# Second and third layer normalisation: the elementwise pass on ScalarE with a scale and a bias for each token

## The chip, the cores and the metric

One core of a Trainium2 chip runs the whole program. The metric is the device time of one execution in microseconds (us). The engines are named as the profile names them: PE is TensorE (matrix multiply), PEld its weight load, DVE is VectorE, ACT is ScalarE, POOL is GpSimd, SP is SyncE, which here only issues DMAs.

## What is computed

2048 tokens (2 batches of 1024) of width 128 go through a feed-forward layer, an attention layer and the same feed-forward layer again; each has a normalisation of x ahead of it and a residual addition behind it. Cut to what matters:

```python
def _layernorm(x, axis=-1, eps=1e-05):
    m = jnp.mean(x, axis=axis, keepdims=True)
    v = jnp.var(x, axis=axis, keepdims=True)
    return (x - m) / jnp.sqrt(v + eps)

x = x + 0.5 * ffn(_layernorm(x), gate_weight, gate_up_proj, down_proj)
x = x + attn(_layernorm(x), W_kv_down, W_k_up, W_v_up, W_q, W_q_rope, W_k_rope, W_o)
x = x + 0.5 * ffn(_layernorm(x), gate_weight, gate_up_proj, down_proj)
```

`ffn` routes each token to the 8 best of 32 experts (logits = x @ gate_weight.T, top 8, softmax weights), gathers up to 128 tokens for each expert, applies the expert and adds the weighted results back to the tokens. `attn` is causal attention with 16 heads, whose keys and values come from a compressed state c_kv = x @ W_kv_down.

## The kernel before, in words

Tokens lie on the 128 partitions, in 16 tiles (`NT`) of 128 tokens, so that x is a tile [128, 16, 128]. The 16 tiles are handled in 4 groups (`NG`) of 4 tiles (`TG`). Each engine has its own program, written out by hand in its final order; the engines wait for each other through semaphores (`wait_ge`, `then_inc`). An engine works strictly in the order of its program, so an instruction that waits holds everything behind it on that engine.

A normalisation m (0, 1, 2) of group i is this on DVE: `stat` (L794, four bn_stats), `moment` (L800, four bn_aggr, which give mean and variance into `mv`), `variance` (L806, adds eps, increments `var_ready`), then on ACT `root` (L539, square root of 4 numbers for each partition into `sd`), then on DVE `norm`: a reciprocal (L812) into `rstd`, and four tensor_scalar (L818), one for each tile, that write xn = (x - mean) * rstd and increment `xn_ready`. The function `front(m)` interleaves these for the first and third normalisation: the norm of group i comes behind the variance of group i+1, and the norm of group 3 stands not in it but in `route(k)` (L914), between `best(k, 0)` and `choice(k, 0)`. The second normalisation is interleaved with the residual additions (`add`, L785) in the loop at L1039 to L1050.

Behind the second normalisation (`transposes(1, xn, compress)` on PE, `transposed(1, after=compressed)` on ACT):

- PE transposes a group of xn (L1182, waits for `xn_ready`) into PSUM, ACT copies it out as `xnT` (`turned_out`, L545), PE multiplies by W_kv_down (`compress`, L1429), ACT copies that out as `ckvT` (`compressed`, L674). PE's order is transpose 0, transpose 1, compress 0, transpose 2, compress 1, transpose 3, compress 2, compress 3, and the transpose of group i waits for the copy of group i-2. PE goes on with `rope` (L1438) only when all four `ckvT` are there.
- ACT's order in this stretch is root of groups 0 to 3 (L667, L668), then the copies.
- A block of matmuls on zeros (`idle_work`, L1172) stands on PE ahead of these transposes.

Behind the third normalisation (k = 1 from here on):

- ACT's order (L740 to L764): roots 0 and 1, `turned_out` of group 0, root 2, `first_part` 0 (L559, the bf16 copy of xn), root 3, `turned_out` 1, `copy_logits` 0 (L563), a table load for Exp with a small activation (`table_for`, L530), `first_part` 1, `turned_out` 2, `copy_logits` 1, `second_part` 0 (L569), and so on.
- PE transposes xn and computes the router's logits for each group (L1200) as soon as `xnT` is there, with a few idle matmuls between.
- DVE's `route` does for each group: `rest_of` (L824, xn minus its bf16 copy), `best` (L833 and L836, top 8 of the logits, waits for `lg_copied`), `choice` (L841, L842, the mask from which PE counts positions). It ends in `active` (L857 to L863), which gives the number of tiles to gather, and `still_hots` (L894), the one-hot matrices that PE's first gather (L1256) takes.
- POOL's `split(1)` (L445) makes the third bf16 part of xn behind `second_part`.

`split_done` counts POOL's splits; the wait for `NG` of it keeps xn of the second normalisation from being written before the first layer has split its own. `x`, `mv`, `rstd` and the new tile are SBUF tiles that stay for the whole kernel.

Of the kernel before, what the change touches and what calls it, by code (L numbers as in the profile page):

```python
# [10 lines left out]
ALU = mybir.AluOpType  # L11
ACT = mybir.ActivationFunctionType
AX = mybir.AxisListType

P = 128
B, T, D = 2, 1024, 128
N = B * T
NT = N // P
# [17 lines left out]
NG = 4  # L36
TG = NT // NG
# [52 lines left out]
ORDER = ((0, 1, 2, 3), YORDER, (0, 1, 2, 3))  # L90
# [16 lines left out]
def build(nc, x_in, w_kv_down, w_k_up, w_v_up, w_q, w_q_rope, w_k_rope, w_o,  # L107
# [3 lines left out]
    def sb(name, shape, dt=F32, stack=None):  # L111
        return (stack or ctx).enter_context(nc.sbuf_tensor(name, shape, dt))

    def sem(name):
        return ctx.enter_context(nc.semaphore(name))
# [11 lines left out]
    with ctx:  # L127
# [7 lines left out]
        x = sb("x", [P, NT, D])  # L135
        xn = sb("xn", [P, NT, D])
# [15 lines left out]
        mv = sb("mv", [P, NT, 2])  # L152
        var = sb("var", [P, NT])
        sd = sb("sd", [P, NT])
        rstd = sb("rstd", [P, NT])
        wat = sb("wat", [P, 5, D])
        wrope = sb("wrope", [P, 2, DR])
        wswap = sb("wswap", [P, 2, DR])
# [105 lines left out]
        w_stored = sem("w_stored")  # L264
        w_back = [sem(f"w_back{c}") for c in range(RING, NCH)]

        stat_done, moments, var_ready, sd_ready, rstd_ready, xn_ready = (
            sem(n) for n in ("stat_done", "moments", "var_ready", "sd_ready", "rstd_ready", "xn_ready"))
        turned, xnT_ready, logits_done = sem("turned"), sem("xnT_ready"), sem("logits_done")
        part0, rem1, part1, split_done = sem("part0"), sem("rem1"), sem("part1"), sem("split_done")  # L270

# [248 lines left out]
        def _(e):  # L520
# [13 lines left out]
            def root(m, i):  # L534

                g = ORDER[m][i]
                t = slice(g * TG, (g + 1) * TG)
                e.wait_ge(var_ready, m * NG + i + 1)
                e.activation(sd[:, t], var[:, t], ACT.Sqrt).then_inc(sd_ready, 1)  # L539

            def turned_out(n, i):

                g = YORDER[i] if n == 1 else i
                e.wait_ge(turned, n * NG + i + 1)
                e.activation(xnT[:, g * BANK:(g + 1) * BANK], ps[:, i % RING, :], ACT.Copy).then_inc(xnT_ready, 1)  # L545

            def transposed(n, after=None):
                for g in range(NG):
                    turned_out(n, g)
                    if after and g >= 1:  # L550
                        after(g - 1)
                if after:
                    after(NG - 1)

            def first_part(k, g):

                t = slice(g * TG, (g + 1) * TG)
                e.wait_ge(xn_ready, 2 * k * NT + (g + 1) * TG)
                e.activation(xp[:, t, 0, :], xn[:, t, :], ACT.Copy).then_inc(part0, 1)  # L559

            def copy_logits(k, g):
                e.wait_ge(logits_done, k * NG + g + 1)
                e.activation(flat(lg[:, g * TG:(g + 1) * TG, :]), ps[:, LBANK[k][g % RING], g * TG * E:(g + 1) * TG * E], ACT.Copy).then_inc(lg_copied, 1)  # L563
# [75 lines left out]
            root(0, 2)  # L639
            first_part(0, 0)  # L640
            turned_out(0, 1)
            root(0, 3)
            copy_logits(0, 0)
# [22 lines left out]
                e.activation(stacked[rows, :], sq[rows, 0, rows], ACT.Copy).then_inc(units_stacked, 1)  # L666
            for g in range(NG):  # L667
                root(1, g)  # L668
            e.wait_ge(w_stored, 32 * (NCH - RING))

            def compressed(i):
# [68 lines left out]
            table_for(ACT.Sqrt)  # L740
            transposed(2)
            root(2, 0)
            root(2, 1)
            turned_out(3, 0)
            root(2, 2)
            first_part(1, 0)
            root(2, 3)
            turned_out(3, 1)
            copy_logits(1, 0)
            table_for(ACT.Exp)  # L750
# [17 lines left out]
        def _(e):  # L768
            e.sem_inc(added, RING)

            def tiles(g):
                return range(g * TG, (g + 1) * TG)

            def group(g):
                return slice(g * TG, (g + 1) * TG)
# [32 lines left out]
            def norm(m, i):  # L808

                g = ORDER[m][i]  # L810
                e.wait_ge(sd_ready, m * NG + i + 1)
                e.reciprocal(rstd[:, group(g)], sd[:, group(g)]).then_inc(rstd_ready, 1)  # L812
                e.wait_ge(rstd_ready, m * NG + i + 1)
                if m >= 1:

                    e.wait_ge(split_done, NG)
                for t in tiles(g):
                    e.tensor_scalar(xn[:, t, :], x[:, t, :], mv[:, t, 0:1], rstd[:, t:t + 1],  # L818
                                    ALU.subtract, ALU.mult).then_inc(xn_ready, 1)

            def rest_of(k, g):

                e.wait_ge(part0, k * NG + g + 1)
                e.tensor_tensor(rem[g][:, :, :], xn[:, group(g), :], xp[:, group(g), 0, :], ALU.subtract).then_inc(rem1, 1)  # L824
# [4 lines left out]
            def best(k, g):  # L829

                e.wait_ge(lg_copied, k * NG + g + 1)
                for t in tiles(g):
                    e.max(t8[:, t, :], lg[:, t, :]).then_inc(top8, 1)  # L833
                e.wait_ge(top8, k * NT + (g + 1) * TG)
                for t in tiles(g):
                    e.match_replace(rep[:, t, :], t8[:, t, :], lg[:, t, :], LOWEST).then_inc(replaced, 1)  # L836

            def choice(k, g):

                e.wait_ge(replaced, k * NT + (g + 1) * TG)  # L840
                e.tensor_scalar(maskb[:, group(g), :], rep[:, group(g), :], TAKEN, None, ALU.is_lt).then_inc(routed, 1)  # L841
                e.tensor_scalar(rep[:, group(g), :], rep[:, group(g), :], TAKEN, UNROUTED, ALU.is_ge, ALU.mult).then_inc(unrouted, 1)  # L842
# [4 lines left out]
            def masked_positions(k, first, last):  # L847

                e.wait_ge(unrouted, k * NG + last)
                e.wait_ge(pos_done, 2 * k + 1 + (first > 0))  # L850
                t = slice(first * TG, last * TG)
                e.tensor_tensor(posm[:, t, :], pos_of(k, first, last), rep[:, t, :], ALU.add).then_inc(posm_ready, 1)
# [46 lines left out]
            def still_hots(c, p, first=0, last=STILL):  # L899

                for t in range(first, last):
                    hot(c, p, t).then_inc(still_ready, 1)
# [6 lines left out]

            def route(k):  # L910

                rest_of(k, 0)
                best(k, 0)
                norm(2 * k, 3)  # L914
                choice(k, 0)
                best(k, 1)
                rest_of(k, 1)
                choice(k, 1)
                best(k, 2)
                rest_of(k, 2)  # L920
                choice(k, 2)
                best(k, 3)
                choice(k, 3)
                rest_of(k, 3)
                masked_positions(k, 0, 1)
                below_best(k)
                masked_positions(k, 1, NG)
                active(k)
                if k == 0:
                    e.wait_ge(bf_consts, 2)  # L930
                e.wait_ge(posm_ready, 2 * k + 2)
                still_hots(0, 0)
# [770 lines left out]
```

## Time and profile before

| what | value |
|---|---|
| runs without a profile | 583.32, 589.75, 589.77 us, median 589.75 us |
| the profiled execution, its own time | 584.68 us |
| span of that execution in the trace | 582.9 us |
| mean granted clock of TensorE | 0.973 of full speed |
| instructions | 11053 |
| busy: PE, DVE, ACT, POOL | 530.4, 423.5, 259.2, 98.8 us |

The page gives the busy time of each engine over the span, the chain of work that ended last (followed back from the last instruction, at each step to what released it), groups of instructions by line, and DMA issues. The trace behind it gives the same for any stretch. All stretches below are in us from the start of the span. What lies between the execution's own time and its span is 1.8 us.

### The profile page before, as it was taken

The numbers are of one execution on the slowest core, as the hardware profiler recorded it, in microseconds if no ns is written. First come the engines' busy times: TensorE is split into PE (matmuls) and PEld (weight loads), VectorE is DVE, ScalarE is ACT, GpSimd is POOL, SyncE is SP. The second block draws the span as 40 slices with busy tenths as digits, with TensorE's granted clock in tenths as the row PEclk, the third lists the DMA queues.
The fourth block names the chain that finished last, engine by engine and source line by source line (L and its number), as shares of the span: only waits on it lengthen the run. The fifth ranks groups of instructions, "written<-read, shape, count | busy, mean of one in ns | idle before, by whom it ended". The sixth has DMA issues, their size and how long they took to land.

```text
span 582.9 us, 11053 instructions
## 1 busy us (share of the span) xinstructions
PE 530.4 (91%) x3538; PEld 330.8 (57%) x3538; DVE 423.5 (73%) x1423; ACT 259.2 (44%) x430; POOL 98.8 (17%) x215
## 2 busy tenths in 40 slices
PE   6989999878886999999999999999998886999995
PEld 2856777743563545555555555545543563577774
DVE  5886888784892777767678676776730499788874
ACT  2843222235423555465645546555477352122222
POOL 2200000012951121121211212121122111000000
PEclk7989999989996999999999999999999998899999
DMA  9994000000251000000000000000000160000002
GB/s 182 179 277 137 24 2 2 1 5 0 87 206 53 2 28 30 28 26 8 24 28 28 29 21 21 18 27 30 1 3 0 59 187 1 1 2 2 2 3 72
DMA packets 25095, 26.70 MB, mean 46 GB/s; under 512 B 6705, under 2 KB 18577, under 8 KB 25041
## 3 DMA queue, kind: packets, MB, share of 16 engines
q1 hardware_dynamic: 24176, 25.63, 16.4%
q8 instruction: 32, 0.52, 0.4%
q10 hardware_dynamic: 864, 0.36, 0.2%
q14 instruction: 23, 0.18, 0.1%
HBM read 17.04 MB, written 8.78 MB: 44 GB/s over the span
## 4 chain that ended last, share of the span: by engine, by line
PE 69%; DVE 15%; POOL 4%; issue 4%; ACT 3%; SPq 2%; DMA 2%; DVEq 0%; POOLq 0%; ACTq 0%
PE ps L1538 12%; PE ps L1602 12%; PE ps L1256 10%; PE ps L1575 9%; PE ps L1342 6%; PE ps L1357 5%; PE ps L1373 3%; DVE summed L1095 2%; PE ps L1534 2%; POOL nl L507 2%; DVE mxh L1098 2%; DVE xn L818 2%; PE ps L1247 2%; ACT probs L729 1%; DVE stats L794 1%
## 5 line engine op out<-in xcount | busy, mean ns | idle before, releaser
L729 ACT ACTIVATE probs<-ps 128x1024 f32<-128x1024 f32 (+2 forms) x192 | 148.2, 809 | 115.6 <-PE ps L1575 115.5
L1098 DVE TENSOR_REDUCE mxh<-ps 128x1 f32<-128x512 f32 (+2 forms) x176 | 117.4, 690 | 49.0 <-PE ps L1538 47.0
L1538 PE MATMUL ps<-Kst,Qst 120*128 120x512 f32 (+3 forms) x384 | 133.0, 412 | 7.1 <-DVE mxh L1098 3.9
L1538 PEld LDWEIGHTS ps<-Kst,Qst 120*128 120x128 f32 x384 | 67.0, 192 | 64.2 <-DVE mxh L1095 23.3
L1575 PE MATMUL ps<-Qst,Kst 121*128 121x512 f32 (+3 forms) x384 | 96.3, 357 | 5.3 <-DMA Qst<-qn_d 3.5
L1095 DVE CUSTOM_DVE_ANT_0 summed<-ps,maskf 128x384 f32<-128x384 f32 (+1 forms) x128 | 76.0, 621 | 20.2 <-PE ps L1538 18.4
L487 POOL TENSOR_SCALAR_AFFINE_SELECT probs<-probs 128x256 f32<-128x256 f32 x128 | 52.3, 409 | 225.6 <-ACT probs L729 225.0
L1602 PE MATMUL ps<-probs,Vst 128*32 128x512 f32 (+3 forms) x768 | 82.2, 500 | 1.2 <-POOL probs L487 1.2
L1575 PEld LDWEIGHTS ps<-Qst,Kst 121*128 121x128 f32 x384 | 67.4, 192 | 26.1 <-issue 10.1
L1256 PE MATMUL ps<-onehot,xp 128*128 128x512 bf16 (+1 forms) x264 | 71.4, 398 | 7.5 <-DVE onehot L894 7.0
L894 DVE TENSOR_SCALAR onehot<-iotab,posm 128x128 bf16<-128x128 bf16 (+1 forms) x352 | 60.4, 250 | 0.2
L1256 PEld LDWEIGHTS ps<-onehot,xp 128*128 128x128 bf16 (+1 forms) x264 | 21.8, 99 | 23.9 <-issue 13.2
L966 DVE TENSOR_SCALAR place<-iota_s,tok 128x768 fp32r<-128x768 f32 x64 | 35.1, 610 | 0.0
L1247 PEld LDWEIGHTS ps<-info,onehot 128*128 128x128 bf16 (+1 forms) x352 | 21.6, 97 | 20.4 <-issue 1.8
L1172 PE MATMUL ps<-zerosb 128*128 128x512 bf16 x103 | 30.6, 416 | 2.4 <-POOL zerosb L427 2.3
L1357 PE MATMUL ps<-bufT,gus 128*96 128x128 f32 x256 | 30.9, 274 | 0.9 <-ACT bufT L588 0.7
L593 ACT ACTIVATE th<-ps 96x512 f32<-96x512 f32 x16 | 9.5, 594 | 49.0 <-PE ps L1357 49.0
L1357 PEld LDWEIGHTS ps<-bufT,gus 128*96 128x96 f32 x256 | 28.8, 163 | 3.4 <-issue 1.6
L1342 PE MATMUL ps<-place,eoh 128*128 128x512 f32 x112 | 29.9, 348 | 0.0
L1602 PEld LDWEIGHTS ps<-probs,Vst 128*32 128x32 f32 x768 | 15.2, 108 | 25.1 <-issue 20.3
L588 ACT ACTIVATE bufT<-ps 128x512 f32<-128x512 f32 x16 | 9.6, 598 | 44.5 <-PE ps L1256 44.5
L1342 PE MATMUL ps<-place,eol 128*128 128x512 f32 x112 | 28.7, 338 | 0.0
(180 smaller groups left out, 608.7 us busy)
## 6 DMA issues: line engine op xcount, KB each, us to landing
wgn<-in_L_ffn_gate_up_proj SPq DMA_DIRECT2D x8, 384.0 KB, 7.5
guT_d<-gus SPq DMA_DIRECT2D x6, 384.0 KB, 2.8
gus<-guT_d SPq DMA_DIRECT2D x6, 384.0 KB, 6.0
Kst<-kn_d SPq DMA_DIRECT2D x28, 64.0 KB
Qst<-qn_d SPq DMA_DIRECT2D x28, 64.0 KB
wdn<-in_L_ffn_down_proj SPq DMA_DIRECT2D x8, 192.0 KB, 8.9
dnT_d<-dns SPq DMA_DIRECT2D x6, 192.0 KB, 3.9
dns<-dnT_d SPq DMA_DIRECT2D x6, 192.0 KB, 6.5
```

The costliest lines, as they stand in the source:

```text
L487: e.affine_select(block, block, [[0, 2], [1, P]], ALU.is_ge, zero, base=0, channel_multiplier=-1).then_inc(masked, 1)
L729: e.activation(probs[n % RING][:, 2 * b:2 * b + 2, lo:BANK], ps[:, 2 * b:2 * b + 2, lo:BANK], ACT.Exp, scale=SCALE).then_inc(probs_ready, 1)
L894: ins = e.tensor_scalar(onehot[p][:, bass.ds(t, 1), q, :].rearrange("p o c -> p (o c)"), iotab[:, :], posm[:, bass.ds(t, 1), c * CE + q:c ...
L966: e.tensor_scalar(place[q][:, :], iota_s[:, 0:NEAR], tok[p][:, q:q + 1], None, ALU.is_equal).then_inc(placed, 1)
L1095: e.tensor_tensor_reduce(summed[m % RING][:, 0:w], s, maskf[:, BANK - w:BANK], 1.0, LOWEST, ALU.add, ALU.max, to).then_inc(mx_ready, 1)
L1098: e.tensor_reduce(to, s.rearrange("p (q k) -> p q k", k=w), AX.X, ALU.max).then_inc(mx_ready, 1)
L1256: ins = e.matmul(ps[:, 0, :], xp[:, bass.ds(t, 1), part, :].rearrange("p o d -> p (o d)"), onehot[p][:, bass.ds(t, 1), :, :].rearrange("p ...
L1342: ins = e.matmul(ps[:, 4 + o // BANK, 0:m], w[p][:, q, :], place[q][:, o:o + m], start=False, stop=False, skip_group_check=True)
L1357: ins = e.matmul(ps[0:F, bank, q * CAP:(q + 1) * CAP], gus[c][:, q, half, :], bufT[p][:, q, :], start=True, stop=True)
L1538: ins = e.matmul(ps[:, bank, i * w:(i + 1) * w], Qst[p][h][0:ROWS, column(b, jt * P):column(b, jt * P) + P], Kst[p][h][0:ROWS, column(b, o ...
L1575: ins = e.matmul(ps[:, 2 * b + h, lo:BANK], Kst[p][h][0:ROWS + 1, column(b, kt * P):column(b, kt * P) + P], Qst[p][h][0:ROWS + 1, column(b ...
L1602: ins = e.matmul(ps[VW * q:VW * (q + 1), 4 + j, lo:BANK], Vst[p][:, b * TB + kt, h, :], probs[n % RING][:, q, lo:BANK], start=(n == OPENS[ ...
```

## The change

The first normalisation stays as it was. For the second and third (m >= 1), DVE's `norm` makes, after the reciprocal, one scalar_tensor_tensor on [128, 4] into a new tile `moved` = (mean * -1) * rstd and returns. The four elementwise instructions go to ACT: a new function `normed(m, i)` waits for `moved_ready` and for `split_done`, and issues four activations with the function Identity, whose scale is a column of `rstd` and whose bias is a column of `moved`: xn = x * rstd - mean * rstd. They increment `xn_ready` as DVE's did. In ACT's program `normed(m, i)` stands right behind `root(m, i)` in every case. In `route(1)` DVE's `norm(2, 3)` moves from behind `best(1, 0)` to the front; `route(0)` is as it was.

```diff
--- before.py
+++ after.py
@@ -153,6 +153,7 @@
         var = sb("var", [P, NT])
         sd = sb("sd", [P, NT])
         rstd = sb("rstd", [P, NT])
+        moved = sb("moved", [P, NT])
         wat = sb("wat", [P, 5, D])
         wrope = sb("wrope", [P, 2, DR])
         wswap = sb("wswap", [P, 2, DR])
@@ -264,8 +265,8 @@
         w_stored = sem("w_stored")
         w_back = [sem(f"w_back{c}") for c in range(RING, NCH)]
 
-        stat_done, moments, var_ready, sd_ready, rstd_ready, xn_ready = (
-            sem(n) for n in ("stat_done", "moments", "var_ready", "sd_ready", "rstd_ready", "xn_ready"))
+        stat_done, moments, var_ready, sd_ready, rstd_ready, moved_ready, xn_ready = (
+            sem(n) for n in ("stat_done", "moments", "var_ready", "sd_ready", "rstd_ready", "moved_ready", "xn_ready"))
         turned, xnT_ready, logits_done = sem("turned"), sem("xnT_ready"), sem("logits_done")
         part0, rem1, part1, split_done = sem("part0"), sem("rem1"), sem("part1"), sem("split_done")
 
@@ -537,6 +538,14 @@
                 t = slice(g * TG, (g + 1) * TG)
                 e.wait_ge(var_ready, m * NG + i + 1)
                 e.activation(sd[:, t], var[:, t], ACT.Sqrt).then_inc(sd_ready, 1)
+
+            def normed(m, i):
+
+                g = ORDER[m][i]
+                e.wait_ge(moved_ready, (m - 1) * NG + i + 1)
+                e.wait_ge(split_done, NG)
+                for t in range(g * TG, (g + 1) * TG):
+                    e.activation(xn[:, t, :], x[:, t, :], ACT.Identity, scale=rstd[:, t:t + 1], bias=moved[:, t:t + 1]).then_inc(xn_ready, 1)
 
             def turned_out(n, i):
 
@@ -666,6 +675,7 @@
                 e.activation(stacked[rows, :], sq[rows, 0, rows], ACT.Copy).then_inc(units_stacked, 1)
             for g in range(NG):
                 root(1, g)
+                normed(1, g)
             e.wait_ge(w_stored, 32 * (NCH - RING))
 
             def compressed(i):
@@ -740,11 +750,15 @@
             table_for(ACT.Sqrt)
             transposed(2)
             root(2, 0)
+            normed(2, 0)
             root(2, 1)
+            normed(2, 1)
             turned_out(3, 0)
             root(2, 2)
+            normed(2, 2)
             first_part(1, 0)
             root(2, 3)
+            normed(2, 3)
             turned_out(3, 1)
             copy_logits(1, 0)
             table_for(ACT.Exp)
@@ -813,7 +827,9 @@
                 e.wait_ge(rstd_ready, m * NG + i + 1)
                 if m >= 1:
 
-                    e.wait_ge(split_done, NG)
+                    e.scalar_tensor_tensor(out=moved[:, group(g)], in0=mv[:, group(g), 0], scalar=-1.0, in1=rstd[:, group(g)],
+                                           op0=ALU.mult, op1=ALU.mult).then_inc(moved_ready, 1)
+                    return
                 for t in tiles(g):
                     e.tensor_scalar(xn[:, t, :], x[:, t, :], mv[:, t, 0:1], rstd[:, t:t + 1],
                                     ALU.subtract, ALU.mult).then_inc(xn_ready, 1)
@@ -909,9 +925,12 @@
 
             def route(k):
 
+                if k == 1:
+                    norm(2, 3)
                 rest_of(k, 0)
                 best(k, 0)
-                norm(2 * k, 3)
+                if k == 0:
+                    norm(0, 3)
                 choice(k, 0)
                 best(k, 1)
                 rest_of(k, 1)
```

## Rows read from the trace of the kernel before

**Rows 1.** Page, parts 1 and 4: busy time by engine, chain that ended last.

```profile
PE 530.4 (91%) x3538; PEld 330.8 (57%) x3538; DVE 423.5 (73%) x1423; ACT 259.2 (44%) x430; POOL 98.8 (17%) x215
...
PE 69%; DVE 15%; POOL 4%; issue 4%; ACT 3%; SPq 2%; DMA 2%; DVEq 0%; POOLq 0%; ACTq 0%
```

**Rows 2.** Timeline of DVE, second normalisation: start us, us, line, operation, out<-in, count.

```profile
123.64 0.17 DVE L806 TENSOR_SCALAR var<-mv 128x4 f32<-128x4 f32 x1
123.71 0.17 DVE L812 RECIPROCAL rstd<-sd 128x4 f32<-128x4 f32 x1
123.92 1.11 DVE L818 TENSOR_SCALAR xn<-x,mv,rstd 128x128 f32<-128x128 f32 x4
...
126.85 0.17 DVE L806 TENSOR_SCALAR var<-mv 128x4 f32<-128x4 f32 x1
...
130.09 1.11 DVE L818 TENSOR_SCALAR xn<-x,mv,rstd 128x128 f32<-128x128 f32 x4
```

**Rows 3.** Timeline of ACT in the same stretch.

```profile
113.85 1.14 ACT L604 ACTIVATE eoh<-ps,wslot 128x128 fp32r<-128x128 f32 x4 [3.12 <-PE ps L1373]
...
120.79 1.28 ACT L539 ACT_TABLE_LOAD   x1
...
123.84 0.21 ACT L539 ACTIVATE sd<-var 128x4 f32<-128x4 f32 x1 [1.55 <-DVE var L806]
...
128.89 1.23 ACT L545 ACTIVATE xnT<-ps 128x512 f32<-128x512 f32 x2
...
135.30 0.60 ACT L674 ACTIVATE ckvT<-ps 128x512 f32<-128x512 f32 x1 [0.41 <-PE ps L1429]
```

**Rows 4.** Timeline of PE in the same stretch.

```profile
129.52 2.07 PE L1429 MATMUL ps<-xnT,wat 128*128 128x512 f32 x2
...
131.94 1.02 PE L1429 MATMUL ps<-xnT,wat 128*128 128x512 f32 x2
```

**Rows 5.** Busy time by stretch (columns in the first line of the view: engines, clock, DMA).

```profile
129.50:131.40 1.90, 1.88 (x3) 0.74 (x4) 1.67 (x7) 0.60 (x1) 0.13 (x1) 0.50 0.00 0
...
133.20:136.00 2.80, 2.07 (x6) 0.53 (x4) 0.00 (x0) 2.09 (x4) 0.29 (x3) 1.00 0.00 0
```

**Rows 6.** Chain that ended last, in order of time: the next consumer.

```profile
136.05 1.96 PE ps L1438 x16
```

**Rows 7.** ACT groups by form, whole kernel: busy us, mean ns of one.

```profile
L604 ACT ACTIVATE eoh<-ps,wslot 128x128 fp32r<-128x128 f32 x64 | 18.3, 369 | 22.7 <-PE ps L1373 22.7
...
L545 ACT ACTIVATE xnT<-ps 128x512 f32<-128x512 f32 x16 | 9.3, 593 | 6.6 <-PE ps L1182 6.5
...
L559 ACT ACTIVATE xp<-xn 128x512 bf16<-128x512 f32 x8 | 5.0, 624 | 0.0
...
L563 ACT ACTIVATE lg<-ps 128x128 f32<-128x128 f32 x8 | 2.2, 275 | 2.0 <-PE ps L1200 2.0
```

**Rows 8.** Busy time by stretch, around the third normalisation.

```profile
462.00:486.00 24.00, 17.95 (x120) 11.50 (x119) 23.44 (x133) 10.48 (x23) 4.75 (x4) 1.00 0.50 149
```

**Rows 9.** Timeline of DVE, third normalisation and routing.

```profile
465.65 0.17 DVE L812 RECIPROCAL rstd<-sd 128x4 f32<-128x4 f32 x1
...
468.15 0.17 DVE L812 RECIPROCAL rstd<-sd 128x4 f32<-128x4 f32 x1
...
474.46 0.48 DVE L833 MAX8 t<-lg 128x8 f32<-128x32 f32 x4
...
484.77 4.15 DVE L894 TENSOR_SCALAR onehot<-iotab,posm 128x128 bf16<-128x128 bf16 x24
```

**Rows 10.** Timeline of ACT in the same stretch.

```profile
471.46 0.28 ACT L563 ACTIVATE lg<-ps 128x128 f32<-128x128 f32 x1 [0.65 <-PE ps L1200]
...
473.16 0.62 ACT L559 ACTIVATE xp<-xn 128x512 bf16<-128x512 f32 x1
...
474.16 0.27 ACT L563 ACTIVATE lg<-ps 128x128 f32<-128x128 f32 x1
```

**Rows 11.** Timeline of PE: first gather of the second expert layer.

```profile
485.77 3.21 PE L1256 MATMUL ps<-onehot,xp 128*128 128x512 bf16 x9 [3.77 <-DVE onehot L894]
```

## The prediction

> **What bounds the kernel now.** I read the page first, for the busy shares and the chain that ended last [rows 1]: PE has 91% of the span and 69% of the chain, DVE 15% of the chain, ACT 3%. So ACT looks like the engine with room, and DVE like the one to relieve. An average over stages decides nothing, though, so I then read the timelines of DVE, ACT and PE and the chain in order of time around the two places that the change touches. What the reader is to see there:
>
> In the second normalisation the chain goes through DVE's additions, statistics and xn blocks, then through PE and ACT alternately (transpose, copy, compress, copy) to the last ckvT copy at 135.30 [rows 3], behind which PE's rope starts at 136.05 [rows 6]. PE has nothing else to do there. In the third, DVE is busy 23.44 of 24 us between 462 and 486 while ACT is busy 10.48 [rows 8]; the chain is DVE's, down to the one-hot matrices at 484.77 [rows 9] and PE's first gather at 485.77 [rows 11]. Both stretches are exposed: PE waits at the end of each, so a delay there is a delay of the end.
>
> **The cost of the moved block.** On DVE four instructions take 1.11 us [rows 2]. On ACT the form with a scale and a bias for each partition from SBUF does not occur. Nearest is the one with a scale alone, 128x128 out of PSUM: 369 ns, and four of them in 1.14 us [rows 3, 7], so one starts (1.14 - 0.37) / 3 = 0.257 us behind the other, an overlap of 0.112. The copy without a pointer of the same size takes 275 ns [rows 7], so a pointer costs 0.094. A 512 wide ACT instruction out of SBUF is 0.031 longer than out of PSUM (624 to 593 [rows 7]). With one pointer more and SBUF as source: 0.369 + 0.094 + 0.031 = 0.494 us each, and with the same overlap 0.382 apart, so the block ends 3 x 0.38 + 0.49 = 1.63 us after it began and ACT can start the next thing after 1.52. Bounds: 0.257 apart, if the second pointer and the source are free in a queue (block 1.1 to 1.3), and 0.494 apart, if nothing overlaps (block 1.98). I take 0.38, the middle, since it rests on rows for each part.
>
> The Trainium skill ("ScalarE: Activation LUTs", section "What ACT_TABLE_LOAD costs") gives 186 ns plus 0.833 for each element, about 93 for each pointer operand, and an overlap of about 93: an estimate by that page is 479 ns each, 386 apart. By it the sum below would not move by more than 0.1 us. The same page's section "Rules for kernel authors" says that multiplications and additions belong on VectorE, which speaks against the change; this trace agrees as far as it can (0.26 us apart on DVE, my 0.38 on ACT).
>
> **The round between the engines.** More than the block's length counts that ACT runs in order. Its program is now root, block, root, block. Root i+1 can't start before block i has been issued, DVE's reciprocal waits for that root, `moved` for the reciprocal, and block i+1 for `moved`. One round: 1.52 (block) + 0.21 (root [rows 3]) + 0.03 (variance's end at 123.81 to root's start at 123.84 [rows 2, 3]) + 0.21 (reciprocal's start to the next instruction's start, 123.71 to 123.92 [rows 2]) + 0.17 (a [128,4] instruction, as the variance [rows 2]) + 0.03 = 2.17 us. Before, the roots ran beside DVE's work and cost the path nothing.
>
> **Second normalisation.** DVE's first reciprocal stays at 123.71, `moved` runs from 123.92 to 124.09, ACT's first block starts at 124.12. DVE is freed of about 0.94 us for each block (1.11 less the small product and its wait), so the variance of group 1's successor comes at 126.85 - 0.94 = 125.91 [rows 2], its partner reciprocal at 125.99, and the second block starts at 125.99 + 0.21 + 0.17 + 0.03 = 126.40: here DVE is just later than ACT. Then the round decides: blocks at 128.57 and 130.74, the last ending at 132.37, where DVE's last block ended at 131.20 [rows 2]. That is only 1.2 us. But behind the blocks on ACT stand the copies, and they were not waiting for the last xn: the first began at 128.89 [rows 3]. It now begins at 130.74 + 1.52 = 132.26, 3.37 later, and compress 0 moves from 129.52 [rows 4] to 132.89. The rest of the alternation keeps its length (6.4 us to the last ckvT's end) but for PE's clock. Between 129.5 and 131.4 it was granted 0.50, its lower level of 1.2 GHz, and from 133.2 on 1.00 [rows 5], after PE had resumed with a transpose at 128.4. Now both first transposes are over by 128.7 and PE idles to 132.9, so a larger part of the alternation runs at the lower level. A compress takes 2.07 us there and 1.02 at the full one [rows 4]; I take half a compress more, 0.5 us. Between 0 and 1.0 is possible. Sum of the stage: 3.4 + 0.5 = 3.9 us later. All that follows (rope, assembly, POOL's copies) hangs on it and nothing covers it. POOL's constants behind `xn_ready` come 1 us later and have time.
>
> **Third normalisation.** The same up to the first reciprocal at 465.65 [rows 9]: block 0 starts at 465.65 + 0.21 + 0.17 + 0.03 = 466.06. Block 1 at + 2.17 = 468.23, issued until 469.75. Now what lies between on ACT counts: the copy xnT 0 (0.49 apart), root 2 at 470.25, block 2 at 470.25 + 0.21 + 0.03 + 0.21 + 0.17 + 0.03 = 470.90, issued until 472.42; first part 0 (0.51); root 3 at 472.93; block 3 at 473.58, issued until 475.10; copy xnT 1 (0.49); and the logits' copy 0 at 475.59, where it was at 471.46 [rows 10]. Then a table load of 1.28, its small activation, first part 1 and xnT 2, as before, and the logits' copy 1 comes at 478.26 instead of 474.16 [rows 10]. DVE saves 0.94 a block and has been relieved of norm 3 between best 0 and choice 0, but it finds no logits: best 0 waits until 475.9, ends at 477.0, and best 1, which began at 474.46 [rows 9], waits for copy 1's end and begins at 478.57. From there to the one-hot matrices DVE has the 10.31 us of work that it had (474.46 to 484.77 [rows 9]), and no wait of its own. So they come at 488.88: 4.1 us later, and the gather with them. PE's idle matmuls hide no work here; should its clock fall while it waits for ACT (it will idle some 2 us before logits 1), up to 1 us more. The read-back of the weights by DMA starts at the same addition as before and has ended when it is wanted.
>
> **The sum.** 3.9 + 4.1 = 8.0 us. On the profiled execution's own 584.68 us this is 592.7 us. The runs without a profile have 589.75 twice and 583.32 once; their median stands 5.07 above the profiled one, and why there are two levels the trace of one execution doesn't tell. Against the median the forecast is 589.75 + 8.0 = 597.8 us, 1.4% slower.
>
> **Rivals.**
> A, not slower: DVE's relief reaches the end. DVE has no idle time in the third stage, and four blocks of 0.94 are 3.8 us. It decides from the point where ACT's round is no longer than DVE's own work for a group: the reciprocals stood 2.50 apart (465.65, 468.15 [rows 9]), 1.56 without the block. For that the block must be at its lower bound (round 2.17 - 0.50 = 1.67, nearly there) and the copies on ACT must keep up. The second stage would still lose 1.9 (copy 0 at 130.8 instead of 128.9). Then - 3.8 + 1.9 = - 1.9: 582.8 by the profiled execution, 587.8 by the median. For it: DVE's 23.44 of 24. Against it: ACT's 10.48 grows by four blocks of 1.5, and its order is fixed.
> B: nothing overlaps on ACT with two pointers. Each of eight blocks costs 0.45 more: 8.0 + 3.6 = 11.6, so 596.3, or 601.4 by the median. For it: no row shows the form. Against: the one-pointer form overlaps as fully as the copy [rows 7].
> C, the change isn't the cheap one it seems: Identity needs another table than Sqrt, and each alternation reloads. Seven loads more in each stage by 1.28 [rows 3] are 18 us on ACT's path: 8.0 + 18 = 26, so 610.7, or 615.8 by the median. For it: Identity occurs nowhere in the trace. Against: copies stand between roots in both stages without a load; the single one of the second stage is at 120.79. The Trainium skill (the same page, section "Table sets: the hidden batching unit") says that identity is in every set; by that rule C can't happen.
>
> **Chances.** Forecast 0.74, A 0.09, B 0.13, C 0.04. The range: the block at 0.257 apart in both stages gives + 1.9 and + 2.1, 588.7 on the profiled execution's level; the upper end is B with the clock's further half, 602, on the median's level. So 588.5 to 602. 2% of 589.75 is 11.8 us, about what a measurement of this kernel can tell from no change. Forecast and A lie within; C and a third of B with bad clocks lie above: slower by over 2% 0.09, faster by over 2% 0.01, within 0.90.
>
> **What would show it right or wrong.** The activations on ACT 0.38 apart and near 0.49 long. Four rounds of 2.2 us in the second stage, DVE idle before each reciprocal; the first xnT copy 3.4 us later than before; the last ckvT 3.9 later. In the third stage DVE idle before best 0 and best 1, released by ACT's logits copies, the one-hot matrices 4.1 later. One table load each, as before. The forecast is wrong if the first copy starts before 131, if best 1 isn't released by ACT, or if the stretch between 143 and 465 changes its length by more than 1 us.

## The result, and the profile after

The changed kernel takes 595.34 us (median of four runs, 593.86 to 597.73) beside 588.19 us for the kernel before (583.32 to 589.77); the ratio is 1.0143, with a 95% interval from 1.0094 to 1.0191. It is 1.4% slower, a difference that the interval keeps clear of zero; its fastest run, 593.86 us, is slower than every run of the kernel before in this document (at most 591.68). The forecast was 597.8 us, 1.4% slower; 1.6 of the 2.5 us by which it lies too high are its starting point, the median of three runs (589.75), which a fourth run lowered to 588.19. The profiled executions are 594.21 and 584.68 us, 9.5 us apart.

The page of the changed kernel, parts 1 and 4:

```profile
span 592.5 us, 11037 instructions
...
PE 532.5 (90%) x3514; PEld 332.5 (56%) x3538; DVE 416.9 (70%) x1399; ACT 271.6 (46%) x462; POOL 98.8 (17%) x215
...
PE 67%; DVE 13%; ACT 5%; issue 5%; POOL 4%; DMA 3%; SPq 2%; DVEq 0%; POOLq 0%; ACTq 0%
```

Against [rows 1], DVE has lost 6.6 us of busy time and ACT has gained 12.4. ACT's share of the chain rose from 3% to 5% and "issue" (the engine waits for nothing that the profile shows) from 4% to 5%. That fits more hand-overs on the path; the timelines below show them.

**Second normalisation.** The profiled executions are not in step here (first reciprocal at 123.15 us, before at 123.71), so I count from that reciprocal. DVE's timeline, columns as in [rows 2]; the bracket gives the idle time before the instruction and what ended it:

```profile
123.15 0.17 DVE L826 RECIPROCAL rstd<-sd 128x4 f32<-128x4 f32 x1
123.35 0.16 DVE L830 SCALAR_TENSOR_TENSOR moved<-mv,rstd 128x4 f32<-128x4 f32 x1
...
127.59 0.18 DVE L826 RECIPROCAL rstd<-sd 128x4 f32<-128x4 f32 x1 [1.32 <-ACT sd L540]
...
129.78 0.18 DVE L826 RECIPROCAL rstd<-sd 128x4 f32<-128x4 f32 x1 [1.81 <-ACT sd L540]
```

ACT's in the same stretch:

```profile
123.55 1.65 ACT L548 ACTIVATE xn<-x,moved,rstd 128x128 f32<-128x128 f32 x4 [1.83 <-DVE moved L830]
...
125.81 1.65 ACT L548 ACTIVATE xn<-x,moved,rstd 128x128 f32<-128x128 f32 x4 [0.52 <-DVE moved L830]
127.37 0.19 ACT L540 ACTIVATE sd<-var 128x4 f32<-128x4 f32 x1
128.00 1.65 ACT L548 ACTIVATE xn<-x,moved,rstd 128x128 f32<-128x128 f32 x4 [0.44 <-DVE moved L830]
...
130.19 1.65 ACT L548 ACTIVATE xn<-x,moved,rstd 128x128 f32<-128x128 f32 x4 [0.44 <-DVE moved L830]
131.75 1.06 ACT L554 ACTIVATE xnT<-ps 128x512 f32<-128x512 f32 x2
...
139.68 0.60 ACT L684 ACTIVATE ckvT<-ps 128x512 f32<-128x512 f32 x1 [0.36 <-PE ps L1448]
```

PE's, to compare with [rows 4], and the busy time by stretch, columns as in [rows 5] (the granted clock is the third number from the end):

```profile
127.61 1.09 PE L1201 MATMUL ps<-sq,xn 128*128 128x128 f32 x4 [1.63 <-ACT xn L548]
132.38 2.08 PE L1448 MATMUL ps<-xnT,wat 128*128 128x512 f32 x2 [3.68 <-ACT xnT L554]
...
135.10 1.92 PE L1448 MATMUL ps<-xnT,wat 128*128 128x512 f32 x2
...
137.66 1.98 PE L1448 MATMUL ps<-xnT,wat 128*128 128x512 f32 x4
```

The stretches:

```profile
128.40:132.30 3.90, 0.29 (x2) 0.00 (x0) 0.34 (x2) 3.46 (x11) 0.40 (x2) 0.50 0.00 0
132.30:137.50 5.20, 5.12 (x12) 2.85 (x13) 0.00 (x0) 2.15 (x5) 1.82 (x6) 0.50 0.00 0
137.50:140.40 2.90, 2.14 (x6) 0.67 (x5) 0.00 (x0) 1.94 (x4) 0.00 (x0) 0.97 0.00 0
```

DVE waits 1.32 and 1.81 us for ACT's root, ACT for DVE's product. Blocks start at 125.81, 128.00 and 130.19. The first copy of xnT comes 8.60 us behind the first reciprocal, where it was 5.18 behind (128.89 - 123.71). The last ckvT comes 16.53 behind, where it was 11.59 behind [rows 3]: 4.9 us more. 3.4 of it are the copy's delay; the other 1.5 are in the alternation that follows, where the first compress takes 2.08 us, as before, but the second still 1.92, while the granted clock is 0.50 from 128.4 up to 137.5. Before, the second took 1.02 [rows 4]. That these 1.5 us belong to the change, and not to this one execution, is not shown: the last section has the same stage without the change.

The ACT group that the change adds:

```profile
L548 ACT ACTIVATE xn<-x,moved,rstd 128x128 f32<-128x128 f32 x32 | 13.2, 485 | 5.9 <-DVE moved L830 5.9
```

**Third normalisation.** DVE and ACT, to compare with [rows 9] and [rows 10], and the busy time of the stretch, to compare with [rows 8]:

```profile
470.83 0.17 DVE L826 RECIPROCAL rstd<-sd 128x4 f32<-128x4 f32 x1
...
475.69 0.18 DVE L826 RECIPROCAL rstd<-sd 128x4 f32<-128x4 f32 x1 [1.80 <-ACT sd L540]
...
478.41 0.18 DVE L826 RECIPROCAL rstd<-sd 128x4 f32<-128x4 f32 x1 [2.34 <-ACT sd L540]
...
481.14 0.47 DVE L849 MAX8 t<-lg 128x8 f32<-128x32 f32 x4 [1.76 <-ACT lg L572]
...
483.83 0.47 DVE L849 MAX8 t<-lg 128x8 f32<-128x32 f32 x4 [1.05 <-ACT lg L572]
...
494.55 3.97 DVE L910 TENSOR_SCALAR onehot<-iotab,posm 128x128 bf16<-128x128 bf16 x24
```

```profile
471.24 1.65 ACT L548 ACTIVATE xn<-x,moved,rstd 128x128 f32<-128x128 f32 x4 [1.32 <-DVE moved L830]
...
480.85 0.26 ACT L572 ACTIVATE lg<-ps 128x128 f32<-128x128 f32 x1
...
483.53 0.27 ACT L572 ACTIVATE lg<-ps 128x128 f32<-128x128 f32 x1
```

```profile
467.00:496.00 29.00, 20.32 (x119) 12.65 (x121) 20.66 (x122) 16.46 (x39) 4.75 (x4) 0.94 0.42 123
```

DVE is idle 1.80 and 2.34 us for roots, then 1.76 and 1.05 us for ACT's copies of the logits. Before, it was busy 23.44 of 24 us; now it is busy 20.66 of 29, and ACT 16.46. The one-hot matrices start 23.72 us behind the stage's first reciprocal, where they started 19.12 behind (484.77 - 465.65): 4.6 us more. Between the last ckvT and this reciprocal lie 331.15 us, before 330.35. So the 9.5 us between the two profiled executions are 4.9 + 0.8 + 4.6, less 0.6 by which this execution was ahead at the first reciprocal and 0.2 in the tail.

### The profile page after: what moved, and what is told of

It is laid out like the page before. It is cut to its first block, busy times and chain, and to the rows that moved or that the text cites. A ratio compares the mean times of both kernels' runs of the same rounds, so it can differ in the third digit from the quotient of the medians.

```text
span 592.5 us, 11037 instructions
## 1 busy us (share of the span) xinstructions
PE 532.5 (90%) x3514; PEld 332.5 (56%) x3538; DVE 416.9 (70%) x1399; ACT 271.6 (46%) x462; POOL 98.8 (17%) x215
## 4 chain that ended last, share of the span: by engine, by line
PE 67%; DVE 13%; ACT 5%; issue 5%; POOL 4%; DMA 3%; SPq 2%; DVEq 0%; POOLq 0%; ACTq 0%
PE ps L1557 12%; PE ps L1621 11%; PE ps L1275 10%; PE ps L1594 9%; PE ps L1361 6%; PE ps L1376 5%; PE ps L1392 2%; PE ps L1553 2%; DVE summed L1114 2%; DMA Qst<-qn_d 2%; POOL nl L508 2%; DVE mxh L1117 2%; ACT xn L548 2%; PE ps L1266 2%; ACT probs L739 1%
## 5 line engine op out<-in xcount | busy, mean ns | idle before, releaser
L1275 PE MATMUL ps<-onehot,xp 128*128 128x512 bf16 (+1 forms) x250 | 68.6, 399 | 8.1 <-DVE onehot L910 6.6
L1191 PE MATMUL ps<-zerosb 128*128 128x512 bf16 x95 | 29.2, 431 | 2.6 <-POOL zerosb L428 2.3
```

The lines of the kernel that those rows point to most:

```text
L1275: ins = e.matmul(ps[:, 0, :], xp[:, bass.ds(t, 1), part, :].rearrange("p o d -> p (o d)"), onehot[p][:, bass.ds(t, 1), :, :].rearrange("p ...
```

## The experiments

The times of the experiments were taken in three groups (each stage alone, roots ahead and idle work in one place; then idle work in two places, the first woven kernel and group 3 only; then the last two), each group on another chip, beside runs of the kernel before on the same chip. The ratios go by those. None of the differences reaches 2%, and those of the third alone and of idle work in one place rest on four runs each. The executions differ by some us from each other for reasons that have nothing to do with the change, as shown below; so for each kernel I read positions in the profile as well, all in us. "Copy", "ckvT", "logits 0", "one-hot" are the start of the first xnT copy and the last ckvT copy behind the second stage's first reciprocal, and of the first logits copy and the one-hot matrices behind the third's. "Rest" is the time from the start of the one-hot matrices to the end of the span:

| kernel | copy | ckvT | logits 0 | one-hot | rest | ratio to before (interval) |
|---|---|---|---|---|---|---|
| before | 5.18 | 11.59 | 5.81 | 19.12 | 98.13 | 1 |
| changed | 8.60 | 16.53 | 10.02 | 23.72 | 97.95 | 1.0143 (1.0094 to 1.0191) |
| only the second | 8.59 | 16.12 | 5.80 | 19.11 | 98.68 | 1.0058 (1.0014 to 1.0102) |
| only the third | 5.17 | 13.13 | 9.99 | 25.34 | 96.56 | 1.0121 (1.0029 to 1.0213) |
| roots ahead | 7.38 | 14.22 | 8.24 | 21.06 | 96.72 | 1.0041 (0.9998 to 1.0083) |
| idle work, one place | 8.59 | 14.71 | 10.00 | 25.36 | 96.77 | 1.0144 (1.0051 to 1.0236) |
| idle work, two places | 8.59 | 14.44 | 10.00 | 22.83 | 98.38 | 1.0046 (1.0011 to 1.0081) |
| copies woven in, second only | 4.22 | 11.58 | 5.81 | 19.11 | 96.74 | 0.9923 (0.9884 to 0.9962) |
| the same, again | 4.22 | 12.44 | 5.80 | 19.11 | 98.94 | 0.9988 (0.9956 to 1.0019) |
| third, group 3 only | 5.18 | 12.92 | 5.81 | 18.49 | 96.97 | 0.9937 (0.9892 to 0.9982) |
| woven and group 3 | 4.22 | 11.58 | 5.80 | 18.48 | 98.24 | 0.9981 (0.9950 to 1.0012) |

**Each stage alone.** The edit, in DVE's norm (shown for the second alone, where `norm(2, 3)` also stands in its old place in `route`; for the third alone it is `m == 2`, and `normed` counts `moved_ready` from this stage on; the calls of `normed` of the other stage are left out):

```diff
-                if m >= 1:
+                if m == 1:
...
                     return
+                if m >= 1:
+                    e.wait_ge(split_done, NG)
```

> Only the second normalisation goes to ACT, the third is as it was. The theory (each stage pays for itself, the second 4.9 us in the changed kernel's trace from its first reciprocal to the last ckvT): 4.4 to 5.7 us over the kernel before, 0.8 to 1.0%. First xnT copy 8.6 us behind the stage's first reciprocal (5.2 before). The rival, that the two delays are not additive because the third stage's ACT work falls on a shifted clock or queue: clearly less or more than half of the whole change's 1.4%.

> Only the third normalisation goes to ACT, the second is as it was. The theory: the one-hot matrices stand 23.7 us behind the third stage's first reciprocal, as in the changed kernel, where they stood 19.1 before; 4.1 to 4.6 us over the kernel before, 0.7 to 0.8%. The second stage's first xnT copy stays 5.2 us behind its first reciprocal. The sum of this run's and the other's excess is the change's 7 to 9.6 us.

Measured: 1.0058, below the expected 1.008 to 1.010 but with an interval up to 1.0102, and 1.0121. The second alone moves only its own positions: the copy to the same place as in the whole change (8.59), the last ckvT to 16.12, 0.4 earlier. The third alone has its first logits copy at the same 9.99, but its one-hot matrices come at 25.34, 1.6 later than the 23.7 expected, and its ratio is above the 1.007 to 1.008 expected, though the interval reaches down to 1.003. Its last ckvT stands at 13.13, though nothing in that stage differs from the kernel before; the last section comes back to it. The two ratios add up to 10.5 us, above the 7 to 9.6 expected for the sum, with intervals of 5 us and more. So each stage's first copy moves by itself and to the same place; the extra 1.6 us was unexplained at this point.

**Is it the round or ACT's load?** Each root one block earlier in ACT's order:

```diff
-            for g in range(NG):
-                root(1, g)
-                normed(1, g)
+            root(1, 0)
+            root(1, 1)
+            normed(1, 0)
+            root(1, 2)
+            normed(1, 1)
+            root(1, 3)
+            normed(1, 2)
+            normed(1, 3)
...
             root(2, 0)
+            root(2, 1)
             normed(2, 0)
-            root(2, 1)
+            root(2, 2)
             normed(2, 1)
...
```

> Same work as in the changed kernel, but each root stands one block earlier on ACT, so that reciprocal and product are made while ACT works on the block before. The theory (a round between two engines in turn, 2.19 us each, of which only 1.55 is ACT's block): blocks then start 1.63 (with a root) or 1.53 (without) apart once DVE is ahead; the first xnT copy 1.2 us earlier behind the stage's first reciprocal (7.4 for 8.6), the third stage's first logits copy 1.8 us earlier (8.2 for 10.0 behind its first reciprocal). Total 2.5 to 3.5 us less than the changed kernel, so 1.0% over the kernel before. The rival, that ACT's throughput alone sets the pace (the blocks' own length): no change, ratio 1.014.

Measured: copy at 7.38 and logits 0 at 8.24, as expected. ACT's timeline of this kernel in the second stage:

```profile
127.18 1.65 ACT L548 ACTIVATE xn<-x,moved,rstd 128x128 f32<-128x128 f32 x4
...
129.44 1.65 ACT L548 ACTIVATE xn<-x,moved,rstd 128x128 f32<-128x128 f32 x4
130.99 0.19 ACT L540 ACTIVATE sd<-var 128x4 f32<-128x4 f32 x1
131.09 3.17 ACT L548 ACTIVATE xn<-x,moved,rstd 128x128 f32<-128x128 f32 x8
134.16 1.05 ACT L554 ACTIVATE xnT<-ps 128x512 f32<-128x512 f32 x2
```

The last two blocks, eight activations, run in one piece of 3.17 us; from the second block on ACT waits for nobody, with the same work as in the changed kernel. So the wait of the two engines for each other costs 1.2 us in the second stage and 1.8 in the third, and ACT's throughput alone is not the pace. The ratio, 1.0041, is lower than the expected 1.010, which its interval doesn't hold. The profile has 2.6 and 1.9 us more than before at the ends of the two stages (14.22 for 11.59, 21.06 for 19.12), together 0.8%, which the interval holds.

**The clock.** Sixteen matmuls on zeros on PE while it waits for ACT, ahead of the first compress:

```diff
                 c = YORDER[i]
+                if i == 0:
+                    idle_work(2, 16)
                 e.wait_ge(xnT_ready, NG + i + 1 + RING)
```

> The changed kernel with 16 matmuls on zeros on PE between the second transpose of the second stage and the first compress, where PE waits 3.7 us for ACT. The theory (of the 4.9 us of that stage 3.4 are ACT's delay and 1.5 are the transposes and compresses at half clock): granted clock 1.00 in the alternation, the last ckvT 1.0 to 1.5 us earlier, 7.4 to 7.9 behind the start of the first xnT copy is 6.4 to 6.9 now; total 1.0 to 2.0 us less than the changed kernel. If the extra 1.5 us come from ACT instead, nothing moves.

PE's timeline:

```profile
129.28 4.97 PE L1191 MATMUL ps<-zerosb 128*128 128x512 bf16 x16
134.08 1.02 PE L1450 MATMUL ps<-xnT,wat 128*128 128x512 f32 x2
...
135.38 1.02 PE L1450 MATMUL ps<-xnT,wat 128*128 128x512 f32 x2
...
136.67 2.03 PE L1450 MATMUL ps<-xnT,wat 128*128 128x512 f32 x4
```

ACT's last copy in the same run:

```profile
138.74 0.60 ACT L684 ACTIVATE ckvT<-ps 128x512 f32<-128x512 f32 x1 [0.41 <-PE ps L1450]
```

The copy stays at 8.59, and the last ckvT comes at 14.71 instead of 16.53. The compresses take 1.02 us each. From the first compress to the last ckvT lie 4.66 us (134.08 to 138.74), where there were 7.30 in the changed kernel's profile and 5.78 before (129.52 to 135.30). So in those two profiles the lower level cost 2.6 and 1.1 us. The last ckvT gains only 1.8, since the sixteen matmuls are too many: the first compress starts 1.46 us behind the start of the first copy, not 0.63.

The total doesn't tell: 1.0144 with an interval from 1.0051, four runs, which holds the 1 to 2 us expected as well as none. And in this execution the third stage's one-hot matrices came at 25.36, as in the run with the third stage alone. In both, the windows show the lower clock over the logits. For the kernel with the third stage alone, the busy time of a stretch over the logits:

```profile
482.00:490.00 8.00, 8.00 (x34) 5.49 (x34) 7.85 (x45) 3.63 (x9) 3.46 (x3) 0.50 0.00 0
```

PE's timeline in the same run:

```profile
478.84 1.08 PE L1220 MATMUL ps<-gateT,xnT 128*128 128x32 f32 x8 [2.10 <-ACT xnT L554]
...
482.12 1.75 PE L1220 MATMUL ps<-gateT,xnT 128*128 128x32 f32 x8
...
484.52 1.75 PE L1220 MATMUL ps<-gateT,xnT 128*128 128x32 f32 x8
```

PE had been idle 2.10 us ahead of the second group's logits. A group of logits takes 1.75 us instead of 1.08, and each pair of idle matmuls between them 1.04 to 1.06 instead of 0.59, so that PE's in-order program falls behind. DVE pays where it takes PE's positions (`posm`):

```profile
492.55 0.56 DVE L869 TENSOR_TENSOR posm<-ps,rep 128x384 f32<-128x384 f32 x1 [1.84 <-PE ps L1253]
```

In the changed kernel's own profile the lower level covered only 482 to 486, and DVE waited not there but only 0.26 us for the third group's logits; that difference is the open 1.6 us. The next run tests that by filling PE's wait as well:

```diff
-            logits(1, 1, 2)
+            logits(1, 1, 12)
```

> The changed kernel with 16 matmuls on zeros ahead of the second stage's first compress and 12 instead of 2 ahead of the third stage's second logits. In the run with the first of these alone the lower clock lay from 478 to 488 us, over the logits, and the one-hot matrices came 25.4 behind the first reciprocal; in the changed kernel's own profile it covered 480 to 484 only and they came at 23.7. The theory (the clock's level over the logits is the difference, and falls because PE waits for ACT ahead of them): the lower clock gone from the logits, one-hot matrices 23.2 to 23.7 behind the first reciprocal, last ckvT 14.7 behind its own. If the 25.4 had another cause, it stays.

(The clock's positions in that text are 2 us early: the windows put the lower level of the run with idle work in one place between 480.2 and 490.4, nearly as in the third stage alone (480.8 to 491), and that of the changed kernel between 482 and 486.) Measured: PE's timeline has it:

```profile
475.86 2.54 PE L1191 MATMUL ps<-zerosb 128*128 128x512 bf16 x11
478.34 1.08 PE L1219 MATMUL ps<-gateT,xnT 128*128 128x32 f32 x8
...
481.02 1.08 PE L1219 MATMUL ps<-gateT,xnT 128*128 128x32 f32 x8
```

The logits stay at 1.08 us, DVE no longer waits for PE's positions, and the one-hot matrices come at 22.83, better than expected and 2.5 us less than without the filler. About 1.9 of these are waits of DVE that are gone; some 0.5 are one `rem` of DVE (L840) that took 1.10 us instead of 1.62, for a reason that stays open. So the 1.6 us left open above were PE at its lower clock.

How much of it reaches the end is another matter. The ratio falls to 1.0046, by which two thirds of the loss would be gone; but the positions of this profile still have 2.9 us more than before at the last ckvT and 3.7 at the one-hot matrices, which is more than the interval holds, and the profile's span is only 0.9 us shorter than with idle work in one place (589.4 for 590.3). The column "rest" shows why: behind the one-hot matrices come 98.4 us here, 96.8 there. Here the granted clock is 0.50 from 490 to 496.6, over the first gathers; there it is 1.00 after 491. Of the 1.6 us that an execution loses over the logits it can get as much back behind them. Between the last ckvT and the third stage's reciprocal both kernels with idle work have 329.4 us, the others 330.3 to 331.2; that is part of the gain and its cause stays open.

**Is it ACT's work or its order?** The first two copies between the blocks, for the second stage alone. The cut is set against the kernel with roots ahead; the third normalisation is as before the change, and the copies behind the blocks keep their order:

```diff
             root(1, 2)
             normed(1, 1)
+            turned_out(1, 0)
             root(1, 3)
             normed(1, 2)
+            turned_out(1, 1)
             normed(1, 3)
```

> Second normalisation on ACT with roots ahead, and the first two xnT copies placed between the blocks (block 0, block 1, copy 0, block 2, copy 1, block 3) instead of behind all four; the third normalisation as before. The theory (the loss was the copies' place in ACT's order, not the 1.55 us that a block costs ACT): first xnT copy 4.2 to 4.5 us behind the stage's first reciprocal (5.2 before, 8.6 changed), last ckvT 11.2 to 12.2 behind it (11.6 before, 16.1 to 16.5 changed), total within 0.3% of the kernel before. The rival, that ACT's total work is too much for this stage whatever its order: last ckvT at 13.5 or later, since four blocks are 6.2 us.

ACT's timeline of this kernel in the second stage:

```profile
126.98 1.65 ACT L548 ACTIVATE xn<-x,moved,rstd 128x128 f32<-128x128 f32 x4
128.53 0.57 ACT L554 ACTIVATE xnT<-ps 128x512 f32<-128x512 f32 x1
...
129.10 1.64 ACT L548 ACTIVATE xn<-x,moved,rstd 128x128 f32<-128x128 f32 x4
130.64 0.58 ACT L554 ACTIVATE xnT<-ps 128x512 f32<-128x512 f32 x1
131.12 1.64 ACT L548 ACTIVATE xn<-x,moved,rstd 128x128 f32<-128x128 f32 x4
...
135.89 0.60 ACT L691 ACTIVATE ckvT<-ps 128x512 f32<-128x512 f32 x1 [0.36 <-PE ps L1455]
```

ACT works without a gap from 126.98 up to the last two copies, which wait 0.26 and 0.36 us for PE. The first copy comes at 4.22, earlier than in the kernel before, and the last ckvT at 11.58, as before. Four blocks on ACT cost this stage nothing if the copies don't stand behind them; the rival, 13.5 or later, falls. The ratio was 0.9923, 4.5 us that no step of the trace showed. I ran the same kernel again:

> The same kernel as the woven one, timed again in more rounds. Its trace showed no step shorter than before by more than a few tenths (last ckvT 11.58 behind the first reciprocal for 11.59), yet its ratio was 0.992. The theory (the trace is right and that ratio was where these runs happened to fall): 0.996 to 1.001. If the woven order gains 4 us that one profile doesn't show: 0.990 to 0.994 again.

It gave 0.9988 (0.9956 to 1.0019), on another chip: no gain that can be told. The two intervals barely touch, so one of them seems too narrow, and a gain below one per cent needs the trace beside it. The two profiles of this one kernel differ by 5.5 us (spans of 582.3 and 587.8): 2.3 arise ahead of the stage's first reciprocal, 0.9 up to the last ckvT, 0.1 up to the third stage and 2.2 behind the one-hot matrices (96.74 for 98.94).

**Relieving DVE where it is the bound.** Of the third stage only group 3 goes to ACT, where the Exp table was loaded:

```diff
             copy_logits(1, 0)
-            table_for(ACT.Exp)
+            normed(2, 3)
...
             copy_logits(1, 3)
+            table_for(ACT.Exp)
```

Groups 0 to 2 and the whole second normalisation are on DVE as before the change, and `norm(2, 3)` stays at the front of `route`. On DVE `rest_of(1, 1)` and `rest_of(1, 2)` go ahead of `best`, and PE's `turn(3, 3, xn, 4)` becomes 2.

> Only group 3 of the third normalisation on ACT, in the place of the Exp table's load, which goes behind the logits' last copy; the bf16 rest of groups 1 and 2 goes ahead of the top 8; two idle matmuls fewer. Everything else as before. The theory (DVE bounds this stage as long as ACT's logits copies come in time): logits' copy 1 8.5 behind the first reciprocal as before, the one-hot matrices 18.1 to 18.4 behind it (19.1 before), total 0.1 to 0.2% less than the kernel before, too little to see in the time. If ACT decides even here, the one-hot matrices come at 19.1 or later.

DVE's timeline of this kernel in the third stage:

```profile
476.00 0.16 DVE L826 SCALAR_TENSOR_TENSOR moved<-mv,rstd 128x4 f32<-128x4 f32 x1
...
478.51 0.69 DVE L838 TENSOR_TENSOR rem<-xn,xp 128x512 f32<-128x512 f32 x1 [0.20 <-ACT xp L568]
...
488.83 3.32 DVE L908 TENSOR_SCALAR onehot<-iotab,posm 128x128 bf16<-128x128 bf16 x20
```

The logits' copy 1 stays in its place (8.52 for 8.51), DVE waits 0.20 us for the bf16 part, and the one-hot matrices come at 18.49: 0.6 us saved, a little less than the 0.7 to 1.0 expected. The edit changes several things at once (the block, the place of the table load, the order on DVE, two idle matmuls), and no run takes them apart. The ratio of 0.9937 is more than 0.6 us can be, and the profile doesn't bear it out.

> The woven second normalisation and group 3 of the third on ACT in one kernel: the version to which the runs point. The theory: last ckvT 11.4 to 11.8 behind its first reciprocal, one-hot matrices 18.4 to 18.7 behind theirs, so 0.5 to 0.8 us less than the kernel before, ratio 0.996 to 1.000, and 0.6 us less than the woven one beside it.

Measured: 11.58 and 18.48, as expected, and 0.9981 (0.9950 to 1.0012). That it is 0.6 us faster than the woven one beside it, as was expected too, can't be told from the times (medians of 585.07 and 586.72 us). The version to which the runs point makes five of the eight blocks on ACT, and the interval leaves it at most 0.12% slower than the kernel before; that it is faster is shown by the positions for 0.6 us and by the times not at all.

## Why the prediction was right

- The block. Expected 0.49 us for one and 1.63 for four; measured 485 ns and 1.65. So the two-pointer form overlaps about as the one-pointer form does (0.097 us for 0.112; rival B falls), and there is one table load in the second stage as before (rival C falls; the roots show no load).
- The round. Expected 2.17; measured 2.19 (125.81 to 128.00 to 130.19). Roots ahead gave the 1.2 and 1.8 us back that this accounts for.
- The order on ACT. Expected: copy 3.37 later, logits 0 4.13 later, logits 1 4.10 later. Measured from the reciprocal: 3.42, 4.21 and 4.19 (483.53 - 470.83 = 12.70 for 8.51). The woven order shows that this is the cause in the second stage, not ACT's work.
- The clock, the term that is least certain. For the second stage the prediction took 0.5 us, "between 0 and 1.0 is possible". The two profiles of before and changed give 1.5, outside that. Its premise, that the clock would rise soon after the first compress began, failed in this execution: the clock was at 0.50 up to about 137.5, 5 us after the compress at 132.38, where before it had risen within 2.1. But from the first compress to the last ckvT the stage without the change took 5.78, 7.33 and 7.11 us in three profiles (before, third alone, group 3 only), and with the change 7.30 and 6.90 in two (changed, second alone). On average that is 0.4 us more, so most of the 1.5 can be the luck of these two executions, and the 0.5 is neither refuted nor shown.
- For the third stage the sum took nothing, and "up to 1 us more" was allowed. The stage without the change ended at 19.11 or 19.12 in four profiles; with it, at 23.72, 25.34 and 25.36, which is 0.5, 2.1 and 2.1 more than the forecast 19.12 + 4.1. Here the lower level over the logits does come with the change, and at the one-hot matrices it was put too low. The two executions that lost most there had 1.2 to 1.6 us less behind them, so up to the end of the span the third stage costs 4.7 us on average (121.9 for 117.2, one-hot and rest together), near the forecast's 4.1.
- The sum. 8.0 us expected; 9.5 between the two profiled executions, 8.4 by the ratio (0.0143 x 588.19). By the averages just named the stages cost 3.4 + 0.4 and 4.7, together 8.5. The mechanism and the 3.4 and 4.1 us of order and round are shown; that the whole came so near has some luck in it, since two profiles of one and the same kernel (the woven one) differ by 5.5 us.
- Rival A. DVE was relieved of 6.6 us and lost them as idle time; that ACT's round decides is borne out by the kernel with roots ahead. With one group of four on ACT, in a place that ACT had for it, the one-hot matrices come 0.6 us earlier; how much of this is the relief is not shown.
- One detail was wrong: DVE was not idle before each of the second stage's reciprocals, only before the last two. The stretch from the last ckvT to the third stage changed by 0.8 us, inside the 1 us that was allowed.

## What to carry to other kernels

An engine with a busy share of 44% is not free at the place where the work goes: what counts is what stands behind the new block on its in-order queue, and who waits for that. Work moved out of a chain of small hand-overs (variance, root, reciprocal, product, block) should be put so that the next link is made while the block runs, and the copies that feed another engine should go between the blocks. If TensorE ends up waiting, count its clock too. Filling the wait with idle matmuls kept the full clock here, but one too many delays the next matmul, and what is gained at one place can be lost behind it: compare the whole span, and more than one profile of each kernel.

## What the runs showed of the hardware

- The clock's part is larger and less even than I had expected. The second stage is the same in the kernel before, in the third stage alone and in group 3 only, and the first copy is at 5.17 to 5.18 in all three; yet the last ckvT comes at 11.59, 13.13 and 12.92. The granted clock was back at 1.00 at 7.9 us behind the first reciprocal in the first of them, 11.1 in the second and 10.7 in the third. The woven kernel, profiled twice, had 11.58 and 12.44, with the clock back 7.2 and 10.4 us behind the reciprocal (at 131.5 and 137.0). Up to 1.5 us of this stage are the clock's from one execution to the next, without any change to the work.
- The same holds behind the one-hot matrices: the "rest" was 96.6 to 97.0 us in five profiles and 98.0 to 98.9 in six, with no order by kernel (the woven kernel has one of each). In the six the windows show a second stretch at the lower level 10 to 20 us behind the one-hot matrices; in the five they show none there.
- The runs of the kernel before spread from 581.6 to 591.7 us over the three groups, not in two levels as the first three times had suggested. In the profiles the first reciprocal of the second stage lies anywhere from 123.15 to 126.84 us, so up to 3.7 us of it arises ahead of everything that these kernels change. All of that arises in the first 37 us: from the first layer's `rden` reciprocal (33.43 to 37.12 us) to this one lie 89.6 to 89.8 us in all eleven profiles. In the four profiles where it comes latest the granted clock stays at 0.50 until 21 to 22 us, in the others it is back at 1.00 by 17. Whether this is the whole of it was not tried.
- An ACTIVATE of 128x128 with scale and bias from SBUF takes 485 ns, four in a row 1.65 us. By the figures of the Trainium skill ("ScalarE: Activation LUTs", section "What ACT_TABLE_LOAD costs") an estimate is 479 ns for one and 386 from one to the next; the trace agrees, with 485 and (1.65 - 0.485) / 3 = 0.388 us.
